# Decoder layer on one core: decay sums from split rows, and eight plain block products for the first pair of both feed-forward stages

## The reference, cut to what matters

```
a = (dt * A).reshape(B, c, Q, H).transpose(0, 1, 3, 2)     # chunks of Q=128 tokens, H=8 heads
cs = jnp.cumsum(a, axis=-1)
Ldec = jnp.where(tri, jnp.exp(cs[..., :, None] - cs[..., None, :]), 0.0)
att = jnp.einsum('bchqn,bchkn->bchqk', Cc, Bc) * Ldec
...
h2 = rmsnorm(h, ln2_w)
mlp = silu(h2 @ gate_w.T) * (h2 @ up_w.T) @ down_w.T       # 1024 -> 3584 -> 1024
...
W = base + mean(|w - base|) * sign(w - base)                # the last part's weights
h = silu(x @ W1.T) * (x @ W3.T);  out = h @ W2.T
```

## Time and profile before

| | |
|---|---|
| runs | 2172.79, 2176.13, 2179.12 us |
| profiled execution | 2173.49 us, span 2171.7 us |
| TensorE busy | 2107.5 us, 97% |
| VectorE busy | 1671.8 us, 77% |
| ScalarE busy | 1071.0 us, 49% |
| GpSimd busy | 182.0 us, 8% |
| mean granted TensorE clock | 0.988 |

### The profile page before, as it was taken

One profiled execution on the slowest core, in us unless ns is written; L12 is line 12 of the kernel. 1 busy time (PEld: TensorE's weight loads), 2 busy tenths in 40 slices (PEclk: granted clock), 3 DMA queues, 4 the chain that ended last, 5 costly groups with the idle time before them and its releaser, 6 DMA issues.

```text
span 2171.7 us, 26574 instructions
## 1 busy us (share of the span) xinstructions
PE 2107.5 (97%) x9222; PEld 1676.7 (77%) x9222; DVE 1671.8 (77%) x2501; ACT 1071.0 (49%) x1760; POOL 182.0 (8%) x296
## 2 busy tenths in 40 slices
PE   6999999979999999999999999799999999999999
PEld 3787778758888888888888854588888888888887
DVE  7775566697777888887979888977777677688885
ACT  4333344456777777774444466533333333444442
POOL 0000110101111111110000002000000000100000
PEclk9999999989999999999999999899999999999999
DMA  3151115627889999989250044544444443755201
GB/s 122 39 187 65 49 49 172 171 53 252 300 304 305 344 332 327 319 305 353 78 194 1 1 155 114 150 162 165 148 170 148 172 151 143 271 204 189 73 20 59
DMA packets 136434, 370.06 MB, mean 170 GB/s; under 512 B 16688, under 2 KB 27568, under 8 KB 132656
## 3 DMA queue, kind: packets, MB, share of 16 engines
q1 hardware_dynamic: 111216, 288.16, 38.9%
q0 software_dynamic: 25088, 80.23, 10.9%
HBM read 288.12 MB, written 84.41 MB: 172 GB/s over the span
## 4 chain that ended last, share of the span: by engine, by line
PE 82%; DVE 11%; ACT 4%; issue 2%; DMA 0%; SPq 0%; DVEq 0%; ACTq 0%
PE pair L934 42%; PE pair L959 24%; PE pair L746 6%; PE pair L739 2%; DVE conv_out L1908 1%; PE pair L990 1%; DVE comb_lo L1660 1%; DVE ring_lo L1609 1%; DVE pair L1746 1%; PE pair L868 1%; PE pair L840 1%; PE pair L847 1%; DVE weights_lo L1524 1%; PE pair L755 1%; PE pair L870 0%
## 5 line engine op out<-in xcount | busy, mean ns | idle before, releaser
L934 PE MATMUL pair<-comb_hi,ring_hi 128*128 128x512 f32 x1568 | 617.4, 394 | 30.2 <-DVE comb_lo L1657 15.6
L934 PE MATMUL pair<-comb_lo,ring_hi 128*128 128x512 f32 x1568 | 615.0, 392 | 0.0
L934 PE MATMUL pair<-comb_hi,ring_lo 128*128 128x512 f32 x1568 | 614.4, 392 | 0.0
L934 PEld LDWEIGHTS pair<-comb_hi,ring_hi 128*128 128x128 f32 x1568 | 297.2, 190 | 100.5 <-issue 17.7
L934 PEld LDWEIGHTS pair<-comb_hi,ring_lo 128*128 128x128 f32 x1568 | 297.3, 190 | 62.4
L959 PE MATMUL pair<-inner_ring_a,ring_hi 128*128 128x512 f32 x1120 | 344.8, 389 | 0.0
L934 PEld LDWEIGHTS pair<-comb_lo,ring_hi 128*128 128x128 f32 x1568 | 297.2, 190 | 61.7 <-issue 0.2
L959 PEld LDWEIGHTS pair<-inner_ring_a,ring_hi 128*128 128x128 f32 x1120 | 210.1, 188 | 43.4
L959 PE MATMUL pair<-inner_ring_a,ring_lo 128*128 128x512 f32 x560 | 217.9, 389 | 0.0
L1183 ACT ACTIVATE ring_hi<-ring_sum 128x512 fp32r<-128x512 f32 x168 | 106.1, 631 | 148.5 <-DVE ring_sum L1596 146.7
L959 PE MATMUL pair<-inner_ring_b,ring_hi 128*128 128x512 f32 x448 | 138.3, 390 | 0.0
(11 more groups left out here) (352 smaller groups left out, 3414.3 us busy)
## 6 DMA issues: line engine op xcount, KB each, us to landing
coeff_in<-f_gu SPq DMA_DIRECT2D x56, 512.0 KB, 5.1
coeff_in<-b_gu SPq DMA_DIRECT2D x56, 512.0 KB, 7.0
weights_raw<-w_mamba SPq DMA_DIRECT2D x44, 512.0 KB, 3.5
raw_a<-w_gu SPq DMA_DIRECT2D x28, 512.0 KB, 7.2
raw_a<-w_gu SPq DMA_DIRECT2D x56, 256.0 KB, 6.1
u_spill<-gate_a POOLq DMA_DIRECT2D x56, 256.0 KB, 6.0
coeff_in<-f_dn SPq DMA_DIRECT2D x28, 512.0 KB, 4.3
coeff_in<-b_dn SPq DMA_DIRECT2D x28, 512.0 KB, 6.2
```

What stands on the lines that cost most here:

```text
L934: ins = pe.matmul(out, wt[:, slot, col], a, start=t in (0, 1, 3) and kk == 0 and n == 0, stop=kk == KH - 1 and n == 2, skip_group_check=True)
```

## The change

It has two parts.

**Decay rows.** The running sums are no longer made again for each chunk on GpSimd and TensorE. After the loop of convolution pairs VectorE copies -cs into three groups of columns (0, 32, 64) of a tile that was set to zero, 72 columns wide. Between the two blocks of the last convolution pair TensorE transposes it with the identity (8 plain float32 matmuls of 128 columns). VectorE then splits the rows in three rounded parts, one in each group of 8 partitions (`decay_rows`, five instructions, put between the two blocks of the last pair). In each chunk GpSimd multiplies these 72 rows by a pick matrix, and TensorE sums them with rounded ones in a single rounded pass.

**First pair.** Pair 0 of both stages is done by eight plain block products (16 turns) on b11, b21, b12 and b22, so that it needs no weight sums and none of t1 to t4. Pair 1 and the following ones are as before. The making and splitting of the combinations is spread over turns 2 to 18. `prefill` has no sums, and for m = 0 fills all seven slots in one go. SyncE's loads of a weight tile wait for the turn that last reads its place.

```diff
+PLAIN = ((0, "b11", 0), (1, "b21", 0), (2, "b11", 2), (3, "b21", 2), (0, "b12", 1), (1, "b22", 1), (2, "b12", 3), (3, "b22", 3))
+NP = 2 * len(PLAIN)
+NG, ND = NP + (PAIRS - 1) * 14, 2 * 7 * SC_PAIRS
+MAKE_AT = ({2: "b22", 3: "t1", 5: "t3", 7: "t2", 10: "t4"},) * 2
+SPLIT_AT = ({6: "b22", 8: "t1", 9: "t3", 15: "t2", 17: "t4"}, {6: "b22", 9: "t3", 15: "t2", 17: "t1", 18: "t4"})
+MOVE_AT = 12
...
             pool.tensor_tensor(
-                cs_rhs[:, :, :], tri.unsqueeze(1).to_broadcast([P, HEADS, P]),
-                a_all[:, b * CHUNKS + c, :].unsqueeze(2).to_broadcast([P, HEADS, P]),
+                cs_rhs[rows, :, :],
+                cs_rows[rows, b * SEQ + c * P:b * SEQ + (c + 1) * P].bitcast(F32).unsqueeze(1).to_broadcast([PARTS_K, HEADS, P]),
+                pick[rows, :].unsqueeze(2).to_broadcast([PARTS_K, HEADS, P]),
                 ALU.mult).then_inc(s_rr, 1)
...
-        conv_pair(CONV_TILES // 2 - 1)
+        conv_block(CONV_TILES // 2 - 1, 0)
+        pe.wait_ge(s_csx, 3)
+        for t in range(NC):
+            ins = pe.matmul(ps[3][0:PARTS_K, t * P:(t + 1) * P], cs_wide[:, t, :], ident, start=True, stop=True)
+        ins.then_inc(s_dtm, 1)
+        conv_block(CONV_TILES // 2 - 1, 1)
...
-                ins = pe.matmul(ps[1][:, g * 512:(g + 1) * 512], ones[:, :], cs_rhs[:, g * HPG:(g + 1) * HPG, :],
+                ins = pe.matmul(ps[1][:, g * 512:(g + 1) * 512], ones_r[0:PARTS_K, :], cs_rhs[0:PARTS_K, g * HPG:(g + 1) * HPG, :],
...
+        def plain(w, m, j, x):
+            pe.wait_ge(s_wlo, w + 1)
+            name, quad = PLAIN[j][1:]
+            out = bank(PLAIN_BANK[quad][x])
+            slot = w % RING
+            for kk in range(KH):
+                if j in (0, 1, 4, 5) and x == 0:
+                    pe.wait_ge(s_tlo, n_lo(m, name, kk))
+                col = slice(kk * P, (kk + 1) * P)
+                hi, lo = part_hi(m, name)[:, kk, :], part_lo(m, name)[:, kk, :]
+                for n, (wt, a) in enumerate(((WRH, hi), (WRH, lo), (WRL, hi))):
+                    ins = pe.matmul(out, wt[:, slot, col], a, start=j % 2 == 0 and kk == 0 and n == 0,
+                                    stop=j % 2 == 1 and kk == KH - 1 and n == 2, skip_group_check=True)
+            ins.then_inc(s_pd, 1)
...
+        def decay_rows():
+            dve.wait_ge(s_dtm, 4)
+            dve.wait_ge(s_spill, 16)
+            top = slice(0, PARTS_K)
+            own.then(dve.tensor_copy(cs_rows[top, :], ps[3][top, :]))
+            own.then(TT(cs_rest[top, :], ps[3][top, :], cs_rows[top, :].bitcast(F32), ALU.subtract))
+            for first in PART_AT[1:]:
+                part = slice(first, first + HEADS)
+                own.then(dve.tensor_copy(cs_rows[part, :], cs_rest[part, :]))
+            TT(cs_rows[part, :], cs_rest[part, :], cs_rows[part, :].bitcast(F32), ALU.subtract).then_inc(s_dte, 1)
...
         conv_pair(2)
+        dve.memset(cs_wide[:, :, :], 0.0)
...
         def feed_forward(m):
-            comb(m, 2)
+            make(m, "b12")
             for w in range(BASE_G[m], W_END[m]):
                 i = w - BASE_G[m]
-                if i < NG and i in (2, 4, 6, 8):
-                    comb(m, i // 2 + 2)
+                if i in MAKE_AT[m]:
+                    make(m, MAKE_AT[m][i])
+                if i in SPLIT_AT[m]:
+                    for kk in range(KH):
+                        part_lo_of(m, SPLIT_AT[m][i], kk)
```

More of the change, by code:

```diff
@@ L131 @@
 N_FORM = len(FORM_NO)
+MAKE_AT = ({2: "b22", 3: "t1", 5: "t3", 7: "t2", 10: "t4"},) * 2
+SPLIT_AT = ({6: "b22", 8: "t1", 9: "t3", 15: "t2", 17: "t4"}, {6: "b22", 9: "t3", 15: "t2", 17: "t1", 18: "t4"})
+LO_PARTS = [["b11", "b21", "b12"] + list(_row.values()) for _row in SPLIT_AT]
+MOVE_AT = 12
+HI_PARTS = [LO_PARTS[0], ["b11", "b21", "b12"] + [n for _, n in sorted([*SPLIT_AT[1].items(), (MOVE_AT, "b22 moved")])]]
+RIGHT = ("b11", "b21", "t2", "t1", "t3", "b22", "t4")
 class Steps:
@@ L426, in build @@
     for m in range(2):
-        for names in (("b11",), ("b21",), ("b22",), ("b12", "t3", "t2"), ("t1",), ("t4",)):
+        for name in ("b11", "b21", "b12", "b22", "t1", "t3", "t2", "t4"):
             for kk in range(KH):
-                for name in names:
-                    made += 1
-                    N_MAKE[m, name, kk] = made
+                made += 1
+                N_MAKE[m, name, kk] = made
     B22_MADE = [N_MAKE[m, "b22", KH - 1] for m in range(2)]
@@ L436, in n_gate, with n_before, n_hi, n_lo @@
         return 4 * pp + order + 1
+    def n_before(pp):
+        return pp - pp // PAIRS - 1
+    def n_hi(m, name, kk):
+        return (m * len(HI_PARTS[0]) + HI_PARTS[m].index(name)) * KH + kk + 1
+    def n_lo(m, name, kk):
+        return (m * len(LO_PARTS[0]) + LO_PARTS[m].index(name)) * KH + kk + 1
+    def part_hi(m, name):
+        if name == "b12":
+            return THr[m][2]
+        return THr[m][3 if name == "b22" and m == 1 else RIGHT.index(name)]
+    def part_lo(m, name):
+        return TLr[m][2 if name == "b12" else RIGHT.index(name)]
+    def value_of(m, name):
+        if name in ("b11", "t2"):
+            return VA[m]
+        return TLf[m][{"b21": 6, "t4": 6, "b22": 5, "b12": 4, "t3": 4, "t1": 3}[name]]
+    PLAIN_BANK = {0: (4, 5), 2: (0, 2), 1: (1, 3), 3: (6, 7)}
     @blk.sync
@@ L566, in _ @@
             load_a22(1, x)
-        for p in range(PAIRS):
+        for x in range(2):
+            load_a1(1, x)
+        for x in range(2):
+            load_a21(1, x)
+        for x in range(2):
+            load_a22(2, x)
+        load_coeff(0)
+        load_coeff(1)
+        for p in range(1, PAIRS):
             for turn in range(14):
+                n = turn_no(p, turn)
                 if turn in (1, 2) and p + 1 < PAIRS:
@@ L1432, in _ @@
                 y_hi(1, KT - 1)
-        for w in range(4, RING):
-            weight_hi(w)
         rms_root(1)
@@ L1537, in _ @@
         dve.memset(coef3[:, :], 0.0)
+        dve.tensor_copy(ones_r[:, :], ones[:, :])
+        own.then(TT(pick[:, :], ident[:, 0:HEADS], ident[:, PART_AT[1]:PART_AT[1] + HEADS], ALU.add))
+        own.then(STT(pick[:, :], pick[:, :], -1.0, ident[:, PARTS_K - HEADS:PARTS_K], ALU.mult, ALU.subtract))
         dve.reciprocal(RS1, X1S)
@@ new lines, in make @@
+        def make(m, name):
+            va = VA[m]
+            for kk in range(KH):
+                dst = value_of(m, name)[:, kk, :]
+                if name in ("b11", "b12", "b21", "b22"):
+                    k = kk if name in ("b11", "b12") else KH + kk
+                    col = 0 if name in ("b11", "b21") else 1
+                    half = COL[m][col]
+                    if m == 0:
+                        ins = STT(dst, hres[:, k, half], par[:, PL2 + k:PL2 + k + 1], rms_scale[:, col, :], ALU.mult, ALU.mult)
+                    else:
+                        ins = TT(dst, xc[:, k, half], scr_c(5)[:, half], ALU.mult)
+                elif name == "t1":
+                    dve.wait_ge(s_tv, N_MAKE[m, "b12", kk])
+                    ins = TT(dst, va[:, kk, :], value_of(m, "b12")[:, kk, :], ALU.subtract)
+                elif name == "t3":
+                    dve.wait_ge(s_tv, N_MAKE[m, "t1", kk])
+                    ins = TT(dst, value_of(m, "b22")[:, kk, :], value_of(m, "b12")[:, kk, :], ALU.subtract)
+                elif name == "t2":
+                    dve.wait_ge(s_tv, N_MAKE[m, "t3", kk])
+                    ins = TT(dst, value_of(m, "t3")[:, kk, :], va[:, kk, :], ALU.add)
+                else:
+                    dve.wait_ge(s_tv, N_MAKE[m, "t2", kk])
+                    ins = TT(dst, va[:, kk, :], value_of(m, "b21")[:, kk, :], ALU.subtract)
+                ins.then_inc(s_tv, 1)
+                if name in ("b11", "b21", "b12") and kk >= 1:
+                    part_lo_of(m, name, kk - 1)
+            if name in ("b11", "b21", "b12"):
+                part_lo_of(m, name, KH - 1)
@@ L1912, in conv_pair @@
                 ins.then_inc(s_conv, 1)
+                if s == 0 and between is not None:
+                    between()
         def scale_hs(ks):
@@ L2174, in _ @@
         ctx_rsqrt(5, bank(7))
-        comb(1, 1)
+        make(1, "b21")
         prefill(1, range(4, RING))
```

342 lines of the change are left out of this document (201 added, 141 removed).

## The result

| | before | changed |
|---|---|---|
| median of the runs | 2176.86 us (2172.79 to 2179.12, 4 runs) | 2154.74 us (2152.86 to 2157.29, 4 runs) |
| profiled execution | 2173.49 us, span 2171.7 | 2155.74 us, span 2153.9 |
| mean granted clock | 0.988 | 0.991 |

The ratio is 0.9903 (95% interval 0.9887 to 0.9919): 22.1 us faster by the medians, 17.8 us by the two profiled executions. Forecast were 25.1 and 2150 us, with a range of 2138 to 2161.

What follows compares the result with a forecast made beforehand. TensorE, busy 97% of the span, was taken as the bound. Scan -8.0, stage 0 -10 and stage 1 -7.1 sum to -25.1 us on 2173.49: 2148.4, 2151.0 on the runs' scale, stated as 2150, range 2138 to 2161.

Steps and rivals of the forecast that it cites:

- The likeliest case: Whole kernel: the forecast itself, 2150 us, within 2145 to 2155, chance 0.48.
- Chunks, 1.27 us each: Scan chunks: two rounded products replace two plain float32 ones, 1.27 us less in each of 8, -10.2 us.
- rival 3: Scan: part one does nothing, chunks held by VectorE and ScalarE, entry's 2.2 us still paid; 2161 us, chance 0.09.
- Scan's entry, +1.8 and +0.4: Before the first chunk: eight plain transposes add 1.8 us, VectorE's zeroing of `cs_wide` adds 0.4 us.
- So nothing on top: Scan's entry: `decay_rows` fits VectorE's idle time before the lo part, adding nothing; bounds 0 and +1.5 us.
- Stage 0: Stage 0's entry: TensorE no longer stopped after `rms_sums(1)`, pair 1 ends earlier; -10 us (-9 to -12.2).
- Rivals 2 and 4: Both stages. 2: VectorE's pace slower, 2157 us, chance 0.17. 4: entry pauses stay whole, kernel slower, 2179 us, chance 0.03.
- Stage 1: Stage 1's entry: VectorE waits 9 us for the sign, TensorE pauses about 6 before turn 9; -7.1 us (-5.6 to -12.1).
- Rival 1: Stage entries: signs and tiles come in time, clock holds; stage 1 -15.9, stage 0 -12.2, total 2140 us, chance 0.20.
- the sign would land only when the queues ran empty: Stage 1's entry: DMA queues full until about 1366.5, so earlier issue gains little; sign lands at 1372.5 (1367.5 to 1374).

Runs made afterwards that it cites:

- e3: Changed kernel with pair 1's `form_weight` in turns 8 to 11 of stage 1 in place of 3, 5, 7 and 9: 2144.37 us.
- e4: Changed kernel with stage 0's sum of squares of the second token half after turn 1, not between turns 0 and 1: 2151.8 us.
- second profile: Changed kernel run again with no edit, beside other follow-up runs: 2156.23 us, ratio 0.99.
- e6: Changed kernel with stage 1's sign loads issued ahead of the `raw_odd` tiles: 2151.1 us, ratio 0.9882.
- e5: Changed kernel with GpSimd's first `cs_rhs` row held until VectorE's last `weights_lo`, and the `cs_wide` memset moved to the kernel's start: 2153.61 us.

## Why the prediction was right, point by point

**The likeliest case held.** 2154.7 against 2150, inside the case's own range of 2145 to 2155. The two stages came as worked out. Two terms of the scan were mis-sized, and its -3.05 us lie outside the bounds of -6.3 to -8.4: the range held because the stages carry most of the sum and the range was wide enough for a miss of 5 us.

- *Chunks, 1.27 us each:* right. Six measured ones gave 1.25 each. The slack of VectorE's state update that was to keep them free did so; rival 3 is out.
- *Scan's entry, +1.8 and +0.4:* mis-sized. From the first mark to the first decay product it costs 103.46 - 98.77 = 4.7 us. The transposes took 1.67 (1.8 forecast) and the memset 0.54 (0.4). On top come 0.70 for VectorE's lo part beside GpSimd, and 1.6 for half clock behind the pause at 144: e3's profile, in which that pause ended at the same distance from the first mark but was 1.10 us long and the clock stayed full, has 101.83, 1.6 less. This half clock came in five of six profiles with the memset there and in none of seven without; it also needs TensorE to be early, as shown above, so it is in part a matter of the execution. I had written "So nothing on top" and looked only at whether GpSimd's row was ready in time, not at what it does to VectorE while it is made.
- *First chunks:* the clock at half behind the pause at 201 cost another 1.6 us (e4 against the changed kernel), and the first product's 1.27 us came as 0.69, since 0.40 us of waiting follow it. The entry is short by 2.5, the second chunk by 1.7, the first product by 0.6 and the other six by 0.1 in all: together the 4.9 us that are missing.
- *Stage 0:* right in its steps. `rms_sums(1)` waited 2.57 us (2.85 forecast) and had the half clock behind it. That was reckoned at 2.2 us and cost 1.6: e4, without the pause and the half clock, comes to turn 16 4.2 us sooner. Turn 16 starts 48.9 us after the stage's first product, 49.4 forecast. No other pause until pair 1 ends. The stage gave the forecast -10 in the second profile and -7.35 in the first. Rivals 2 and 4 are out.
- *Stage 1:* right in every step. VectorE waits 8.97 us (9), for the sign; TensorE pauses 6.43 us (about 6) before turn 9; turn 16 starts 55.5 us after the stage's first product (55.0 forecast). Rival 1 fell with it, and e3 shows what it would have been worth: 10 us in this stage. What I hadn't seen is that the signs needed no such late issue (e6).

**The pages behind it.** That the sign would land only when the queues ran empty came true: share 1.06 and 1.00 until 1360, 0.45 with the landing, as before at 1372.5. The sign was issued earlier than before and landed 10.7 us later in place of 7.4, which is 30.2 us after the stage's first product in both. The Trainium skill, "DMA: Bandwidth & Descriptors", section "Queues, rings and completion order", has each DMA engine serve its queues in turn; the landing agrees with that, though no row shows the turns.

For the mis-sized term the row was there to be read. VectorE's 1.93 in place of 1.23 us came while GpSimd worked from 192.21 to 194.10, and with GpSimd moved behind it (e5) it took 1.23 again. The Trainium skill, "SBUF — State Buffer", section "SBUF: two separate sides", says that VectorE and GpSimd share a pair of ports under an exclusive lock, and that a VectorE operation with two SBUF inputs blocks against a GpSimd operation that reads SBUF. This trace agrees in kind: `weights_lo` is such an operation. A full block from 193.26 to 194.10 would have made it 2.07 us, 1.93 was measured.

## What to carry to other kernels

When work moves on an engine that had slack, look at what it runs beside, not only at whether its result is in time: 1.9 us of GpSimd cost VectorE 0.7 us and TensorE's pause as much. A pause of about 2 us on TensorE can have a second price, half clock behind it: taking away two delays of 0.54 and 0.70 us gained 1.2 us where the clock was the same with and without them, and 2.9 where they also brought half clock (e5). A short pause in one trace may be a long one in the next execution, so a delay added there isn't priced by one row. A load needed early is best issued before the ones that wait: SyncE issues in program order, and the signs stood behind tiles that they had nothing to do with.
